# The second layers' sums over d on ScalarE, and three in place of four GpSimd products for the odd streams' third layer

## The chip, the cores and the metric

The kernel runs on one core of a Trainium2 chip. The metric is the device time of one execution in microseconds, with everything from the load of the ids to the store of the result. The profile is one execution of the same program on the chip, and times in it are counted from the start of its span.

## What is computed

A batch of 1024 samples looks up one row of 16 numbers in each of 32 tables (`e`, 1024 x 32 x 16). A compressed interaction network of three layers runs on it, and its sums go with 16 dense features through three dense layers:

```python
x0 = xk = e                                   # b, m = 32, d = 16
for W in (W0, W1, W2):                        # W: 32 x h x 64, h = 32, 64, 64
    xk = relu(einsum('bmd,bhd,mhk->bkd', x0, xk, W))
    outs.append(sum(xk, axis=2))              # the sum over d: b x 64
z = concatenate(outs, axis=1)                 # b x 192
h = relu(concatenate([z, dense_ctx], axis=1) @ W_top1 + b_top1)
h = relu(h @ W_top2 + b_top2)
y = h @ W_top3
```

Everything is float32.

## The kernel before

**Streams and tiles.** The batch is cut into 16 streams of 64 samples (`STREAMS`). Streams 2t and 2t+1 form tile t and share the dense layers; below, a is the even stream of a tile, b the odd one. Even streams use slot 0 of every double buffer, odd ones slot 1 (`s = stream % 2`). The 64 samples times 16 values of d are the 1024 columns of every large tile.

**Layers and chunks.** A layer is a sum over chunks of 128 pairs (m, h): first an elementwise product of `rolled` (rotated copies of x0, 128 x 1024 each, loaded by DMA) and of the layer's input, then two matmuls (one for each half of the columns) of the 64 columns of weights of that chunk, which add up in a PSUM bank of `acc`. The first layer has 4 chunks and one chunk of squares, the second and the third have 16 each. The profile shows four matmul records for a chunk.

**Who makes the products.** VectorE makes most, two chunks at a time into one of three buffers `zd` (128 x 2048 at L406, input `xk_ps` in PSUM); where the number of its chunks in a part is odd, the last instruction has one chunk. GpSimd makes the others, one at a time into four buffers `zg` (L335, input `xk_sb` in SBUF). Between its products GpSimd issues the indirect gathers of the embedding rows (L323), as many after each product as the table `GATHERS_AFTER` says. `CHUNKS[slot, layer]` is a list of parts, each a pair (chunks of VectorE, chunks of GpSimd).

**Order.** The parts are run by TensorE and VectorE in the order of the list `ORDER`. In the steady state a tile t is

```python
ORDER += [(2 * _t - 1, 2, 0), (2 * _t, 0, 0), (2 * _t - 1, 2, 1), (2 * _t, 1, 0), (2 * _t + 1, 0, 0),
          (2 * _t, 1, 1), (2 * _t + 1, 1, 0), (2 * _t, 2, 0)]
```

with entries (stream, layer, part), layers counted from 0. The stream b- = 2t-1 of the tile before finishes its third layer inside this tile. `PLAN.merged` says in which order TensorE takes the products of the two engines. VectorE may be three buffers ahead of TensorE at most: each product waits for `zd_used` of the product three before it.

**After a layer.** ScalarE waits for the layer's last matmul and evacuates `acc` with relu into `xk_ps` and `xk_sb` (L472, four activations of 64 x 512 each), which the next layer's products read (`evacuate`). For the sum over d there are two ways. For the third layers, except that of the last stream, ScalarE makes it itself from PSUM (`sum_d`, L451: 32 activations of 128 x 16 with an accumulated output, each followed by a reading of the accumulator). For the others ScalarE writes relu of the bank to `relu_ab` in SBUF (L481) and VectorE reduces that (L382, `reduce_d`), placed so many products later as `SUMS_AFTER` says for the layer. The function `by_act` says which way a layer goes.

**Banks.** The first layers use bank 2 of `acc`, the second and third layers of a stream use bank s. So the third layer of a stream can't start on TensorE until the second layer's bank has been read for the last time: L563 waits for `relu_ready`, which the L481 activation gives.

**ScalarE's order** is written out by hand from L504: in a tile t copy of the base for a (`base_to_ps`), squares, `sum_d(a - 2)`, evacuate (a, 0), the same for b, then the copies of the dense layers (`zsum_to_sb`, `h1_to_sb`), evacuate (a, 1), `h2_to_sb`, `y_to_sb`, evacuate (b, 1).

## Time and profile before

| what | value |
|---|---|
| median of 3 runs | 620.88 us (619.57 to 621.36) |
| the profiled execution, its time | 619.78 us |
| its span in the profile | 618.0 us |
| TensorE matmuls, share of the span busy | 91% |
| VectorE | 90% |
| GpSimd | 76% |
| ScalarE | 48% |
| granted TensorE clock, mean | 0.994 |

Of two engines that pass buffers to each other, the one that sets the pace is the one that the other waits for. Both TensorE and VectorE are nearly always busy here, so the table alone doesn't say which it is: that is read stretch by stretch from the idle time that stands in square brackets behind the rows of the timeline, with the engine whose work ended it. ScalarE's records of `sum_d` overlap each other in time, so their busy time and mean durations are larger than the time that a sum takes.

### The profile page before, as it was taken

What the parts mean: (1) busy time and instruction counts of PE and PEld (TensorE: products, weight loads), DVE (VectorE), ACT (ScalarE), POOL (GpSimd) and SP (SyncE); (2) the same over time, 40 slices, a digit from 0 to 9 for tenths busy, and PEclk for the clock granted to TensorE, in tenths of its full rate; (3) what the DMA queues carried; (4) which work ended last, traced back from release to release, by engine and by line L of the source; (5) the groups of instructions that cost most, each with busy time, mean ns of one, the idle gap of its engine ahead of it and who ended that gap; (6) DMA issues with size and microseconds to landing.
All of it is one profiled execution on the core that took longest, in us unless ns stands there. A gap on an engine that the chain in (4) does not pass through costs nothing.

```text
span 618.0 us, 8180 instructions
## 1 busy us (share of the span) xinstructions
PE 562.0 (91%) x2752; PEld 206.1 (33%) x2752; DVE 554.5 (90%) x281; ACT 299.5 (48%) x1366; POOL 468.6 (76%) x354
## 2 busy tenths in 40 slices
PE   0058889999999999999999999899998999999997
PEld 0012222334333443334333433234332433334334
DVE  0067899999999999999999999989998999999991
ACT  0021607574357535674366535674346544774331
POOL 6748888888888888888888888888888885125450
PEclk9998999999999999999999999999999999999999
DMA  6297979792699819893699719793498809892000
GB/s 171 79 382 254 394 250 396 241 397 82 209 359 330 294 51 374 297 399 108 218 351 339 299 40 379 265 400 130 171 397 309 329 3 319 316 406 100 1 2 0
DMA packets 54252, 152.02 MB, mean 246 GB/s; under 512 B 9697, under 2 KB 18913, under 8 KB 54210
## 3 DMA queue, kind: packets, MB, share of 16 engines
q1 hardware_dynamic: 46018, 149.39, 64.7%
q0 software_dynamic: 8192, 2.11, 2.6%
q8 instruction: 21, 0.34, 0.2%
q14 instruction: 21, 0.17, 0.1%
HBM read 147.26 MB, written 4.20 MB: 245 GB/s over the span
## 4 chain that ended last, share of the span: by engine, by line
PE 48%; POOL 23%; DVE 10%; issue 9%; DMA 6%; SPq 1%; ACT 1%; DVEq 0%; POOLq 0%
PE acc L570 43%; POOL emb L323 14%; DVE zd L406 10%; POOL zg L335 9%; DMA rolled<-x_scratch 5%; PE mlp L613 2%; SPq L287 1%; PE mlp L604 1%; PE mlp L605 1%; PE acc L579 1%; PE mlp L620 0%; DVE zpart L382 0%; PE mlp L586 0%; ACT xk_sb L472 0%; DMA emb<-tables_in,index 0%
## 5 line engine op out<-in xcount | busy, mean ns | idle before, releaser
L406 DVE TENSOR_TENSOR zd<-rolled,xk_ps 128x2048 f32<-128x2048 f32 x239 | 530.0, 2279 | 16.2 <-PE acc L570 9.2
L570 PE MATMUL acc<-zd,w_sb 128*64 128x512 f32 x1672 | 384.6, 597 | 8.4 <-DVE zd L406 8.4
L323 POOL DMA_INDIRECT emb<-tables_in,index x256 | 244.6, 955 | 75.3 <-issue 64.3
L335 POOL TENSOR_TENSOR zg<-rolled,xk_sb 128x1024 f32<-128x1024 f32 x94 | 223.8, 2382 | 52.0 <-ACT xk_sb L472 18.9
L570 PEld LDWEIGHTS acc<-zd,w_sb 128*64 128x64 f32 x1672 | 119.7, 138 | 242.5 <-issue 210.4
L472 ACT ACTIVATE xk_sb<-acc 64x512 f32<-64x512 f32 x128 | 75.7, 591 | 64.4 <-PE acc L570 61.9
L570 PE MATMUL acc<-zg,w_sb 128*64 128x512 f32 x376 | 98.6, 601 | 6.9 <-POOL zg L335 6.9
L570 PE MATMUL acc<-zd,w 128*64 128x512 f32 x256 | 61.6, 601 | 37.4 <-DVE zd L406 37.4
L472 ACT ACTIVATE xk_ps<-acc 64x512 f32<-64x512 f32 x126 | 71.8, 570 | 30.1 <-PE acc L570 27.2
L451 ACT ACTIVATE relu_ab<-acc 128x16 f32<-128x16 f32 x480 | 78.9, 294 | 8.3 <-PE acc L570 8.3
L451 ACT ACTIVATION_READ_ACCUMULATOR relu_ab<-acc 128x1 f32 x480 | 79.3, 322 | 0.0
L434 ACT ACTIVATE xk_sb<-base 128x1024 f32<-128x1024 f32 x16 | 16.9, 1056 | 67.6 <-PE acc L570 39.2
L570 PEld LDWEIGHTS acc<-zg,w_sb 128*64 128x64 f32 x376 | 26.9, 137 | 58.3 <-issue 41.8
L570 PEld LDWEIGHTS acc<-zd,w 128*64 128x64 f32 x256 | 18.7, 139 | 74.3 <-issue 71.6
L430 ACT COPY xk_ps<-base 128x512 f32<-128x512 f32 x30 | 16.6, 587 | 45.4 <-DVE zd L406 28.2
L406 DVE TENSOR_TENSOR zd<-rolled,base 128x1024 f32<-128x1024 f32 x4 | 4.9, 1225 | 27.9 <-DMA rolled<-x_scratch 27.7
L382 DVE TENSOR_REDUCE zpart<-relu_ab 128x32 f32<-128x512 f32 x33 | 22.3, 677 | 5.2 <-ACT relu_ab L481 5.2
L491 ACT ACTIVATE h<-mlp,bt 128x128 f32<-128x128 f32 x28 | 8.0, 368 | 38.8 <-PE mlp L605 38.8
L481 ACT ACTIVATE relu_ab<-acc 128x512 f32<-128x512 f32 x33 | 19.7, 597 | 9.4 <-PE acc L570 8.6
L502 ACT COPY z2d_y<-mlp 1x128 f32<-1x128 f32 x7 | 1.8, 254 | 36.4 <-PE mlp L620 36.4
L579 PE MATMUL acc<-xk_sb,w 128*64 128x512 f32 x64 | 17.2, 613 | 0.0
L613 PEld LDWEIGHTS mlp<-h,wt 128*128 128x128 f32 x112 | 13.0, 191 | 5.7 <-issue 5.7
(45 smaller groups left out, 101.0 us busy)
## 6 DMA issues: line engine op xcount, KB each, us to landing
rolled<-x_scratch SPq DMA_DIRECT2D x256, 512.0 KB, 9.4
base<-x_scratch SPq DMA_DIRECT2D x16, 512.0 KB
emb<-tables_in,index POOLq DMA_INDIRECT x256
x_scratch<-emb SPq DMA_DIRECT2D x32, 128.0 KB
w_sb<-w_in SPq DMA_DIRECT2D x2, 512.0 KB, 4.9
wt<-wtop_in SPq DMA_DIRECT2D x1, 512.0 KB, 6.3
wt1a<-wtop_in SPq DMA_DIRECT2D x1, 256.0 KB, 5.5
w<-w0a_in SPq DMA_DIRECT2D x1, 160.0 KB, 2.3
```

The source lines that it names most:

```text
L323: pool.indirect_dma_start(emb[:, i % 2, c * DIM:(c + 1) * DIM], None, tables, bass.IndirectOffsetOnAxis(index[:, g:g + 1].bitcast(U32), 0) ...
L335: nc.gpsimd.tensor_tensor(zg[:, n % ZG_BUFS, :], rolled[:, s, j, :], xk_sb[:, s, :], ALU.mult).then_inc(zg_ready, 1)
L382: nc.vector.tensor_reduce(zpart[:, t % 2, layer, s, :], relu_ab[:, s, :].rearrange("p (b d) -> p b d", d=DIM), AX_X, ALU.add).then_inc(red ...
L406: nc.vector.tensor_tensor(zd[:, n % ZD_BUFS, 0:w, :], rolled[:, s, j:j + w, :], repeated(layer_in, w), ALU.mult).then_inc(zd_ready, 1)
L430: nc.scalar.copy(xk_ps[:, s, h * HALF:(h + 1) * HALF], base[:, h * HALF:(h + 1) * HALF]).then_inc(base_ps, 1)
L434: nc.scalar.activation(xk_sb[:, i % 2, :], base[:, :], ACT.Square).then_inc(squares_ready, 1)
L451: end = nc.scalar.activation(relu_ab[:, s, cols], acc[:, s, cols], ACT.Relu, accum_out=zpart[:, t % 2, 2, s, b:b + 1])
L472: nc.scalar.activation(dst[copy * MAPS:(copy + 1) * MAPS, s, h * HALF:(h + 1) * HALF], acc[h * MAPS:(h + 1) * MAPS, bank, :], ACT.Relu).th ...
L481: nc.scalar.activation(relu_ab[:, s, :], acc[:, bank, :], ACT.Relu).then_inc(relu_ready, 1)
L570: end = nc.tensor.matmul(acc[h * MAPS:(h + 1) * MAPS, bank, :], weights, z[:, h * HALF:(h + 1) * HALF], start=(j + c == 0), stop=(i == len ...
L579: nc.tensor.matmul(acc[h * MAPS:(h + 1) * MAPS, bank, :], w0[:, L0CH, :], xk_sb[:, s, h * HALF:(h + 1) * HALF], start=False, stop=False)
L613: end = nc.tensor.matmul(mlp[:, c * TB:(c + 1) * TB], wt2[:, k, c * P:(c + 1) * P], h1[:, k, :], start=(k == 0), stop=(k == H1 // P - 1))
```

## The change

Two things change in one step. First, `by_act` is true of the second layers too: their sum over d is made by `sum_d` on ScalarE, the L481 activation and VectorE's reduction of these 16 layers fall away, and TensorE's third layers wait for `summed` in place of `relu_ready`. Second, the second part of an odd stream's third layer goes from (8, 3) to (9, 2): VectorE makes nine chunks of it, the ninth in an instruction of its own, and GpSimd two. (The last stream has a row of its own in `CHUNKS_AT` and keeps its split, so this is seven streams.) The seven gathers that stood after three products, as 2, 2 and 3, stand after two, as 3 and 4.

```diff
@@ -44,7 +44,7 @@
 
 
 CHUNKS = {(0, 0): [(4, 0)], (0, 1): [(4, 0), (10, 2)], (0, 2): [(12, 4)],
-          (1, 0): [(4, 0)], (1, 1): [(14, 2)], (1, 2): [(4, 1), (8, 3)]}
+          (1, 0): [(4, 0)], (1, 1): [(14, 2)], (1, 2): [(4, 1), (9, 2)]}
 
 CHUNKS_AT = {(0, 1): [(14, 2)], (0, 2): [(6, 1), (8, 1)], (STREAMS - 1, 2): [(12, 4)]}
 
@@ -54,12 +54,12 @@
               (2 * _t, 1, 1), (2 * _t + 1, 1, 0), (2 * _t, 2, 0)]
 ORDER += [(STREAMS - 1, 2, 0)]
 
-SUMS_AFTER = [5, 5, 4]
+SUMS_AFTER = {0: 5, 2: 4}
 
 
 GATHERS_FIRST = 24
 GATHERS_EARLY = 8
-GATHERS_AFTER = {(0, 1, 1): [3, 3], (1, 1, 0): [3, 3], (0, 2, 0): [3, 3, 2, 2], (1, 2, 0): [3], (1, 2, 1): [2, 2, 3]}
+GATHERS_AFTER = {(0, 1, 1): [3, 3], (1, 1, 0): [3, 3], (0, 2, 0): [3, 3, 2, 2], (1, 2, 0): [3], (1, 2, 1): [3, 4]}
 GATHERS_AFTER_AT = {(0, 1, 0): [4, 7], (0, 2, 0): [3], (1, 1, 0): [3, 4], (0, 2, 1): [7],
                     (STREAMS - 1, 2, 0): [0, 0, 0, 0]}
 
@@ -113,12 +113,17 @@
 
 def by_act(stream, layer):
 
-    return layer == 2 and stream < STREAMS - 1
+    return layer > 0 and (stream, layer) != (STREAMS - 1, 2)
 
 
 def sums_to(stream, layer):
 
     return sum(last_part(q) and not by_act(*ORDER[q][:2]) for q in range(end_of(stream, layer) + 1))
+
+
+def act_sums_to(stream, layer):
+
+    return sum(last_part(q) and by_act(*ORDER[q][:2]) for q in range(end_of(stream, layer) + 1))
 
 
 def phase_before(stream, layer):
@@ -438,18 +443,20 @@
                 who, n, _, _ = PLAN.merged[end_of(stream, layer)][-1]
                 act.wait_ge(zd_used if who == "dve" else zg_used, n + 1)
 
-            def sum_d(stream):
-
-                s, t = stream % 2, stream // 2
-
-                act.wait_ge(reduced, sums_to(stream, 1))
+            def sum_d(stream, layer):
+
+                s, t, bank = stream % 2, stream // 2, bank_of(stream, layer)
+
+                act.wait_ge(reduced, sums_to(stream, layer - 1))
+                if layer == 2:
+                    act.wait_ge(summed, act_sums_to(stream, 1))
                 if t > 1:
 
                     act.wait_ge(zsum_done, t - 1)
                 for b in range(SH):
                     cols = slice(b * DIM, (b + 1) * DIM)
-                    end = nc.scalar.activation(relu_ab[:, s, cols], acc[:, s, cols], ACT.Relu,
-                                               accum_out=zpart[:, t % 2, 2, s, b:b + 1])
+                    end = nc.scalar.activation(relu_ab[:, s, cols], acc[:, bank, cols], ACT.Relu,
+                                               accum_out=zpart[:, t % 2, layer, s, b:b + 1])
                 end.then_inc(summed, 1)
 
             def evacuate(stream, layer):
@@ -472,12 +479,12 @@
                                 nc.scalar.activation(
                                     dst[copy * MAPS:(copy + 1) * MAPS, s, h * HALF:(h + 1) * HALF],
                                     acc[h * MAPS:(h + 1) * MAPS, bank, :], ACT.Relu).then_inc(ready, 1)
-                if layer > 0:
-
-                    act.wait_ge(reduced, sums_to(stream, layer - 1))
-                elif stream > 1:
-
-                    act.wait_ge(summed, stream - 1)
+                if by_act(stream, layer):
+                    return
+                before = phase_before(stream, layer)
+                if before:
+
+                    act.wait_ge(summed, act_sums_to(*before))
                 nc.scalar.activation(relu_ab[:, s, :], acc[:, bank, :], ACT.Relu).then_inc(relu_ready, 1)
 
             def zsum_to_sb(m):
@@ -507,29 +514,33 @@
             base_to_ps(1)
             squares(1)
             evacuate(0, 1)
+            sum_d(0, 1)
             evacuate(1, 0)
             evacuate(1, 1)
+            sum_d(1, 1)
             act.wait_ge(const_in, const_count)
             for t in range(1, TILES):
                 a, b, m = 2 * t, 2 * t + 1, t - 1
                 base_to_ps(a)
                 wait_end(a - 2, 2)
                 squares(a)
-                sum_d(a - 2)
+                sum_d(a - 2, 2)
                 evacuate(a, 0)
                 base_to_ps(b)
                 wait_end(b - 2, 2)
                 squares(b)
-                sum_d(b - 2)
+                sum_d(b - 2, 2)
                 evacuate(b, 0)
                 zsum_to_sb(m)
                 h1_to_sb(m)
                 evacuate(a, 1)
                 h2_to_sb(m)
+                sum_d(a, 1)
                 y_to_sb(m)
                 evacuate(b, 1)
+                sum_d(b, 1)
             wait_end(STREAMS - 2, 2)
-            sum_d(STREAMS - 2)
+            sum_d(STREAMS - 2, 2)
             evacuate(STREAMS - 1, 2)
             act.wait_ge(last_z01_done, 1)
             nc.scalar.copy(z01[:, :], stage[:, 0:TB]).then_inc(last_z01_sb, 1)
@@ -558,9 +569,9 @@
                 if layer == 0 and stream > 0:
                     pe.wait_ge(relu_ready, sums_to(stream - 1, 0))
                 elif layer == 1 and part == 0 and stream > 1:
-                    pe.wait_ge(summed, stream - 1)
+                    pe.wait_ge(summed, act_sums_to(stream - 2, 2))
                 elif layer == 2 and part == 0:
-                    pe.wait_ge(relu_ready, sums_to(stream, 1))
+                    pe.wait_ge(summed, act_sums_to(stream, 1))
                 for i, (who, n, j, w) in enumerate(merged):
                     pe.wait_ge(zd_ready if who == "dve" else zg_ready, n + 1)
                     for c in range(w):
@@ -589,8 +600,8 @@
 
             def zsum(m):
 
-                pe.wait_ge(reduced, sums_to(2 * m + 1, 1))
-                pe.wait_ge(summed, 2 * (m + 1))
+                pe.wait_ge(reduced, sums_to(2 * m + 1, 0))
+                pe.wait_ge(summed, act_sums_to(2 * m + 1, 2))
                 if m > 0:
                     pe.wait_ge(y_ready, m)
                 half_sums(m, mlp[0:MAPS, 0:TB], 0)
@@ -625,7 +636,8 @@
             pe.wait_ge(const_in, const_count)
             def last_sums():
 
-                pe.wait_ge(reduced, sums_to(STREAMS - 1, 1))
+                pe.wait_ge(reduced, sums_to(STREAMS - 1, 0))
+                pe.wait_ge(summed, act_sums_to(STREAMS - 1, 1))
                 half_sums(TILES - 1, stage[0:MAPS, 0:TB], 0)
                 half_sums(TILES - 1, stage[MAPS:P, 0:TB], 1).then_inc(last_z01_done, 1)
 
@@ -642,7 +654,7 @@
 
             m = TILES - 1
             pe.wait_ge(last_z01_sb, 1)
-            pe.wait_ge(summed, STREAMS - 1)
+            pe.wait_ge(summed, act_sums_to(STREAMS - 2, 2))
             for c in range(H1 // P):
                 nc.tensor.matmul(last_h1_bank[c], wt1a[:, c * P:(c + 1) * P], z01[:, :], start=True, stop=False)
             pe.wait_ge(y_ready, m)
```

What stands on ScalarE in the first tile, from stream 0's second layer to stream 1's second layer. Before (two `evacuate` blocks, each ended by L481, then the start of the third):

```order
L472 ACTIVATE xk_sb<-acc 64x512 x4
L472 ACTIVATE xk_ps<-acc 64x512 x4
L481 ACTIVATE relu_ab<-acc 128x512
L472 ACTIVATE xk_sb<-acc 64x512 x4
L472 ACTIVATE xk_ps<-acc 64x512 x4
L481 ACTIVATE relu_ab<-acc 128x512
```

After (L458 is `sum_d`, L479 the evacuations, L488 what was L481):

```order
L479 ACTIVATE xk_sb<-acc 64x512 x4
L479 ACTIVATE xk_ps<-acc 64x512 x4
L458 ACTIVATE relu_ab,zpart<-acc 128x16 x32
L479 ACTIVATE xk_sb<-acc 64x512 x4
L479 ACTIVATE xk_ps<-acc 64x512 x4
L488 ACTIVATE relu_ab<-acc 128x512
```

The 32 small activations stand between the evacuation of stream 0's second layer and that of stream 1's first layer, where one activation stood.

What stands on VectorE in one steady turn, from behind the reduction of the first layer of one b to that of the next. Before (the reductions are those of (a, 1), (b, 1), the next (a, 0) and the next (b, 0)):

```order
L406 TENSOR_TENSOR zd<-rolled,xk_ps 128x2048 x5
L382 TENSOR_REDUCE zpart<-relu_ab 128x32
L406 TENSOR_TENSOR zd<-rolled,xk_ps 128x2048 x7
L382 TENSOR_REDUCE zpart<-relu_ab 128x32
L406 TENSOR_TENSOR zd<-rolled,xk_ps 128x2048 x10
L382 TENSOR_REDUCE zpart<-relu_ab 128x32
L406 TENSOR_TENSOR zd<-rolled,xk_ps 128x2048 x8
L382 TENSOR_REDUCE zpart<-relu_ab 128x32
```

After, the same turn (L387 is the reduction, L411 the products):

```order
L411 TENSOR_TENSOR zd<-rolled,xk_ps 128x2048 x21
L411 TENSOR_TENSOR zd<-rolled,xk_ps 128x1024
L387 TENSOR_REDUCE zpart<-relu_ab 128x32
L411 TENSOR_TENSOR zd<-rolled,xk_ps 128x2048 x9
L387 TENSOR_REDUCE zpart<-relu_ab 128x32
```

Of four reductions in the tile two are left, those of the first layers, and one product of half the width is new. It stands before the reduction of (a, 0), at the end of part (b-, 2, 1).

What TensorE takes in the part (b-, 2, 1) and the part (a, 1, 0) behind it (here stand two matmuls for a chunk; `zd` are VectorE's chunks, `zg` GpSimd's), before:

```order
L570 MATMUL acc<-zd,w_sb 64x512 x4
L570 MATMUL acc<-zg,w_sb 64x512 x2
L570 MATMUL acc<-zd,w_sb 64x512 x4
L570 MATMUL acc<-zg,w_sb 64x512 x2
L570 MATMUL acc<-zd,w_sb 64x512 x4
L570 MATMUL acc<-zg,w_sb 64x512 x2
L570 MATMUL acc<-zd,w_sb 64x512 x12
```

and after:

```order
L581 MATMUL acc<-zd,w_sb 64x512 x8
L581 MATMUL acc<-zg,w_sb 64x512 x2
L581 MATMUL acc<-zd,w_sb 64x512 x8
L581 MATMUL acc<-zg,w_sb 64x512 x2
L581 MATMUL acc<-zd,w_sb 64x512 x10
```

TensorE has the same number of chunks; the third product of GpSimd is gone from the place before the last ones, and both that are left come later.

## Rows read from the trace of the kernel before

**Rows 1.** the page, busy time of each engine and its share of the span

```profile
PE 562.0 (91%) x2752; PEld 206.1 (33%) x2752; DVE 554.5 (90%) x281; ACT 299.5 (48%) x1366; POOL 468.6 (76%) x354
```

**Rows 2.** timeline of VectorE, one steady tile; start, duration, what, idle before

```profile
229.13 8.88 DVE L406 TENSOR_TENSOR zd<-rolled,xk_ps 128x2048 f32<-128x2048 f32 x4 [0.48 <-PE acc L570]
237.93 0.68 DVE L382 TENSOR_REDUCE zpart<-relu_ab 128x32 f32<-128x512 f32 x1
238.53 22.05 DVE L406 TENSOR_TENSOR zd<-rolled,xk_ps 128x2048 f32<-128x2048 f32 x10
...
290.26 0.68 DVE L382 TENSOR_REDUCE zpart<-relu_ab 128x32 f32<-128x512 f32 x1
...
298.49 8.88 DVE L406 TENSOR_TENSOR zd<-rolled,xk_ps 128x2048 f32<-128x2048 f32 x4 [0.48 <-PE acc L570]
```

**Rows 3.** timeline of TensorE, one steady tile

```profile
248.66 1.89 PE L570 MATMUL acc<-zd,w 128*64 128x512 f32 x8
...
272.22 1.94 PE L570 MATMUL acc<-zd,w_sb 128*64 128x512 f32 x8 [0.22 <-DVE zd L406]
```

**Rows 4.** timeline of TensorE, its waits for GpSimd in two later tiles

```profile
329.89 1.08 PE L570 MATMUL acc<-zg,w_sb 128*64 128x512 f32 x4 [0.55 <-POOL zg L335]
...
401.10 1.08 PE L570 MATMUL acc<-zg,w_sb 128*64 128x512 f32 x4 [1.67 <-POOL zg L335]
```

**Rows 5.** timeline of VectorE, the same place in the first and last tiles

```profile
159.77 8.88 DVE L406 TENSOR_TENSOR zd<-rolled,xk_ps 128x2048 f32<-128x2048 f32 x4 [0.48 <-PE acc L570]
...
510.58 8.88 DVE L406 TENSOR_TENSOR zd<-rolled,xk_ps 128x2048 f32<-128x2048 f32 x4 [0.48 <-PE acc L570]
...
580.03 8.88 DVE L406 TENSOR_TENSOR zd<-rolled,xk_ps 128x2048 f32<-128x2048 f32 x4 [0.49 <-PE acc L570]
```

**Rows 6.** groups by shape: products and gathers; busy us, mean ns, idle before

```profile
L406 DVE TENSOR_TENSOR zd<-rolled,xk_ps 128x2048 f32<-128x2048 f32 x239 | 530.0, 2279 | 16.2 <-PE acc L570 9.2 <-DMA rolled<-x_scratch 6.3 <-ACT xk_ps L472 0.3
...
L323 POOL DMA_INDIRECT emb<-tables_in,index x256 | 244.6, 955 | 75.3 <-issue 64.3 <-DVE zd L406 6.1 <-DVE index L365 2.6
L335 POOL TENSOR_TENSOR zg<-rolled,xk_sb 128x1024 f32<-128x1024 f32 x94 | 223.8, 2382 | 52.0 <-ACT xk_sb L472 18.9 <-PE acc L570 18.2 <-DMA rolled<-x_scratch 13.2
...
L406 DVE TENSOR_TENSOR zd<-rolled,base 128x1024 f32<-128x1024 f32 x4 | 4.9, 1225 | 27.9 <-DMA rolled<-x_scratch 27.7
```

**Rows 7.** timeline of GpSimd, first wait but issue after 73.69

```profile
503.94 2.37 POOL L335 TENSOR_TENSOR zg<-rolled,xk_sb 128x1024 f32<-128x1024 f32 x1 [0.42 <-PE acc L570]
```

**Rows 8.** timeline of ScalarE, one steady tile, with one sum

```profile
235.69 0.60 ACT L481 ACTIVATE relu_ab<-acc 128x512 f32<-128x512 f32 x1
240.84 1.11 ACT L430 COPY xk_ps<-base 128x512 f32<-128x512 f32 x2 [4.54 <-DVE zd L406]
...
245.54 0.17 ACT L451 ACTIVATE relu_ab<-acc 128x16 f32<-128x16 f32 x1
...
250.45 0.45 ACT L451 ACTIVATION_READ_ACCUMULATOR relu_ab<-acc 128x1 f32 x1
...
290.79 0.62 ACT L497 ACTIVATE h<-mlp,bt 128x128 f32<-128x128 f32 x2 [1.68 <-PE mlp L613]
```

**Rows 9.** timeline of ScalarE, first tile

```profile
69.45 0.60 ACT L481 ACTIVATE relu_ab<-acc 128x512 f32<-128x512 f32 x1
71.17 2.44 ACT L472 ACTIVATE xk_sb<-acc 64x512 f32<-64x512 f32 x4 [1.13 <-PE acc L570]
73.64 2.35 ACT L472 ACTIVATE xk_ps<-acc 64x512 f32<-64x512 f32 x4
```

**Rows 10.** timeline of VectorE, first tile

```profile
76.06 0.68 DVE L382 TENSOR_REDUCE zpart<-relu_ab 128x32 f32<-128x512 f32 x1
76.65 4.47 DVE L406 TENSOR_TENSOR zd<-rolled,xk_ps 128x2048 f32<-128x2048 f32 x2
...
103.61 0.68 DVE L382 TENSOR_REDUCE zpart<-relu_ab 128x32 f32<-128x512 f32 x1
```

**Rows 11.** the chain that ended last, its end

```profile
578.12 26.76 PE acc L570 x124
```

## Prediction

> **What bounds the kernel now.** The page comes first: TensorE is busy for 91% of the span, VectorE for 90%, GpSimd for 76%, ScalarE for 48% [rows 1]. Two engines near 90% that hand buffers to each other can't be told apart by that, so the second view is the timeline of VectorE over one steady tile. It has one place where VectorE waits for TensorE with all three buffers full, 0.48 us before the product at 229.13, and it comes back at 298.49, one tile of 69.36 us later [rows 2]. From there VectorE runs without a gap, and it is TensorE that catches up: its one wait for a product in that tile is at 272.22 [rows 3]. Then TensorE is ahead until the next full point. So each tile has two stretches. From the full point to 272.22 the end is set by VectorE's chain; from 272.22 to the next full point it is set by TensorE alone, and time taken from VectorE there buys nothing.
>
> VectorE's chain can be counted. Ten products start in 238.53 to 260.50, 2.197 us each, and a reduction moves the next start by 0.60 us (237.93 to 238.53) [rows 2]. From 229.13 to the product that TensorE waits for stand 19 products and two reductions: 19 x 2.197 + 1.20 = 42.94, which gives 272.07. TensorE starts at 272.22 [rows 3]. The count holds.
>
> The third view is the same full point over the whole run. From 159.77 to 298.49 two tiles take 69.36 us each, but the six tiles from 159.77 to 580.03 take 420.26 [rows 2, 5], where six of the steady kind would take 416.16. The 4.10 us between them stand on TensorE as waits for GpSimd's third product of part (b-, 2, 1): 0.55 us in tile 4, 1.67 in tile 5 [rows 4], and once more as much in tile 6. GpSimd doesn't wait for anyone from its product at 73.69 to 503.94 [rows 7]: it falls behind slowly, since its gathers (0.955 us plus 0.29 idle) and its products (2.38 us) take more than a tile in tiles 1 to 5 [rows 6]. Behind 578.12 TensorE runs 124 records without a gap [rows 11], so at the end it is the bound, and one chunk (four records) costs it 0.86 us.
>
> **What the change does, part by part.**
>
> *GpSimd, one product fewer in each of seven tiles.* A product with its gap is 2.4 to 2.7 us (2.38 alone; with the mean idle of a gather, 0.29, added [rows 6]); I take 2.5. At the wait of 0.55 us in tile 4 three products are saved, 7.6 us. Against that stands a delay of some 3.4 us that the change brings in the first tile (below), since GpSimd's product there reads what ScalarE writes later. The 4.2 us left exceed 0.55, and a tile later 6.7 exceed 1.67. The waits go: -4.1 us. I give this nearly its full size; the least would be zero.
>
> *VectorE in the steady tiles.* Of the 19 products and two reductions on its chain, one reduction leaves (the one at 237.93, -0.60). The other that leaves stands at 290.26 [rows 2], in the stretch where TensorE sets the end, and brings nothing. The new product of half the width comes on the chain. No row has it with this input. The four single products of the first layer take 1225 ns where a double takes 2279 [rows 6], so a single is 1.054 shorter: 2.197 - 1.054 = 1.14 us. The bounds are 1.05 (the columns alone) and 1.23 (the whole record). Without the reduction VectorE reaches the buffer of the last product of (a, 2) slightly before TensorE has freed it: TensorE ends that part 5 chunks before 248.66, at 244.37 [rows 3], and VectorE would start on that buffer 0.07 us too early. So a tile gets longer by 1.14 - 0.60 + 0.07 = +0.6 us (0.45 to 0.75). Six full tiles lie between 159.77 and 580.03: +3.6 us. The seventh single product is in the first tile.
>
> *ScalarE in the steady tiles.* A sum starts at 245.54 and its last reading of the accumulator starts at 250.45 [rows 8]: 5.0 us for 32 pairs, 5.4 with the end of the last record. The mean durations of these records can't be added, since they overlap. The sum of (b, 1) takes the place of the activation at 235.69 and ends at 240.8 to 241.1. Three things stand behind it: TensorE's part (b-, 2, 0) at 244.37, 3.3 us later; the base copies, which began at 240.84, take 1.1 us and are needed by VectorE seven products after 229.13, at 244.5; and the squares, which wait for TensorE at 244.4 anyway. The sum of (a, 1) starts behind the copy at 290.79 and ends at 296.8; TensorE wants that bank 16 chunks before 244.37, at 230.6, which is 300.0 in this tile, 3.2 us later. Cost in the steady tiles: nothing, with 3 us of cover in each.
>
> *The first tile.* Here there is no such cover. The activation at 69.45 becomes a sum of 5.1 us, and stream 1's evacuation, which began at 71.17 and ended at 75.99 [rows 9], can start only at 74.55 and ends at 79.4. VectorE's part (1, 1, 0) needs it, and began at 76.65 [rows 10]: +2.75 us, with the reduction at 76.06 already taken out. TensorE's (0, 2, 0) is late by three microseconds too, but TensorE was waiting for VectorE in this stretch. From here to the first steady point VectorE's chain sets the pace: the reduction at 103.61 [rows 10] leaves (-0.60) and the first single product comes (+1.14). The sum of (1, 1) ends about 107.5, a microsecond before VectorE needs the base copies behind it. Together +3.3 us (3.1 with the shortest sum and single, 3.8 with the longest).
>
> *The end.* TensorE is the bound and its work is the same: 0.
>
> **Sum.** +3.3 + 3.6 - 4.1 = +2.8 us on the span of 618.0. The profiled execution took 619.78, so 1.78 lie around the span, and 622.6 is its successor. The median of the runs before is 1.10 above the profiled one; so the forecast for the median is 623.7 us.
>
> **What the notes say.** The Trainium skill (Perfetto Trace Analysis, Identifying the Most-Contended Engine) says to take occupancy as the measure and to relieve the engine that has most of it; by that VectorE, with 9.6 us of reductions gone and 8.0 us of single products new, is relieved, by 1.6 us. The first rival below is this rule put to work, and gives 615.2 us where my sum gives 623.7; the trace speaks against it, since the relief at 290.26 falls where VectorE waits. The Trainium skill (ScalarE: Activation LUTs, Rules for kernel authors) budgets about 0.3 us for each ACTIVATE, which would make a sum 10 us; the trace has 5.0, and this rule stands beside the third rival.
>
> **Rivals.**
> 1. *VectorE's total decides.* If what counts is VectorE's whole work and not its place, 16 reductions (16 x 0.60 = 9.6) leave and seven singles (8.0) come: -1.6, and with the GpSimd waits gone -5.7, 615.2 us. It decides if VectorE keeps what it gains at 290.26 over the full point, and if its lead covers the late evacuation of the first tile. Against it: the wait of 0.48 at every full point, and 0.6 us of lead where 2.75 are wanted. Chance 7%.
> 2. *One of the two losses isn't there*: the first tile is covered (3.6 - 4.1), or the tiles keep 69.36 (3.3 - 4.1). Then 620.1 to 620.4 us, no change to be measured. Chance 17%.
> 3. *The sums are late in every tile.* This needs a sum of more than 8.3 us. With 10 us each the two streams wait 1.7 and 1.8 us in each of seven tiles and the first tile loses 5 more: 623.7 + 24 + 5 = 653. For it speaks only that no row shows a sum with other work queued straight behind it. Chance 5%.
> 4. *GpSimd's waits stay*, because it loses its lead again to waits of its own: 623.7 + 4.1 = 627.8. It would have to lose 4 us before tile 4. Chance 4%.
>
> My forecast has the other 67%.
>
> **How the numbers follow.** A difference of 0.3% is 1.9 us, about what a measurement of this kernel can tell. The forecast's own range is 622.2 to 625.2: the bounds of the single product (7 x 0.1), of the sum (0.4) and the scatter of the median (0.9). Rival 2 with some scatter brings the low end to 619.8, and half of rival 4 the high end to 626.3. Faster is rival 1 and a little of rival 2: 0.10. Same is most of rival 2 and a small part of the forecast, whose lower edge lies at 1.3 above the median of before: 0.22. Slower is the rest: 0.68.
>
> **What the new profile would show.** In a steady tile, the full point on VectorE comes back after 69.9 to 70.1 us in all tiles alike, and TensorE has no waits for GpSimd. TensorE's wait for VectorE ahead of (a, 1, 1) is about 0.9 us in two or three pieces in place of 0.22 to 0.38. VectorE's first product of (1, 1, 0) stands at 79.4 behind a wait for ScalarE. GpSimd shows waits from the middle on. I would be wrong if TensorE waits for ScalarE's sum in the steady tiles, if the full points stay 69.4 apart, or if a single product costs about as much as a double.

## The result, and the profile of the changed kernel

The changed kernel took 627.25 us (median of six runs, 624.82 to 629.62), the kernel before beside it 619.91 us (619.11 to 621.36). The ratio is 1.0113, with a 95% interval of 1.0086 to 1.014: slower by 1.1%. The forecast was 623.7 us with a range up to 626.3, so the sign was right and the size was not: 7.3 us lost where 2.8 were forecast. (The 620.88 us of the table above are the median of three of the six executions that give 619.91.) The profiled execution has a span of 625.5 us and took 627.29.

The page of the changed kernel, busy time of each engine, answers to [rows 1]:

```profile
PE 568.2 (91%) x2752; PEld 206.7 (33%) x2752; DVE 553.6 (89%) x272; ACT 377.9 (60%) x2374; POOL 451.4 (72%) x347
```

The work moved as the diff says. ScalarE has 78 us more, GpSimd 17 us less, VectorE about the same. TensorE has the same 2752 matmuls and 6 us more of busy time, a first sign that its clock wasn't always full.

The timeline of VectorE, changed kernel, first tile and its full point, answers to [rows 10] and the first of [rows 5]:

```profile
79.38 4.49 DVE L411 TENSOR_TENSOR zd<-rolled,xk_ps 128x2048 f32<-128x2048 f32 x2 [3.63 <-ACT xk_ps L479]
83.78 0.68 DVE L387 TENSOR_REDUCE zpart<-relu_ab 128x32 f32<-128x512 f32 x1
84.38 24.25 DVE L411 TENSOR_TENSOR zd<-rolled,xk_ps 128x2048 f32<-128x2048 f32 x11
110.10 4.49 DVE L411 TENSOR_TENSOR zd<-rolled,xk_ps 128x2048 f32<-128x2048 f32 x2 [1.47 <-ACT xk_ps L435]
115.32 6.68 DVE L411 TENSOR_TENSOR zd<-rolled,xk_ps 128x2048 f32<-128x2048 f32 x3 [0.74 <-PE acc L581]
...
165.50 29.91 DVE L411 TENSOR_TENSOR zd<-rolled,xk_ps 128x2048 f32<-128x2048 f32 x14 [0.48 <-PE acc L581]
```

The first wait is the one that was forecast, at the forecast time, 79.4. The second (1.47 us, for the base copies behind the sum of (1, 1)) and the third (0.74 us, for TensorE) were not. The full point is at 165.50 where it was at 159.77: 5.73 us lost in the first tile, forecast 3.3.

The same engine's full points in the later tiles, changed kernel, answer to [rows 2, 5]:

```profile
203.36 13.28 DVE L411 TENSOR_TENSOR zd<-rolled,xk_ps 128x2048 f32<-128x2048 f32 x6 [0.43 <-DMA rolled<-x_scratch]
...
306.93 29.80 DVE L411 TENSOR_TENSOR zd<-rolled,xk_ps 128x2048 f32<-128x2048 f32 x14 [1.02 <-PE acc L581]
...
376.83 29.91 DVE L411 TENSOR_TENSOR zd<-rolled,xk_ps 128x2048 f32<-128x2048 f32 x14 [0.48 <-PE acc L581]
...
587.53 4.49 DVE L411 TENSOR_TENSOR zd<-rolled,xk_ps 128x2048 f32<-128x2048 f32 x2 [0.48 <-PE acc L581]
```

The six tiles take 587.53 - 165.50 = 422.03 us, 1.77 more than before; the forecast was 0.5 less. The tile from 306.93 to 376.83 has the forecast length, 69.90 (69.96 was said). Others are longer: the first has two waits for a DMA (0.23 and 0.43 us), and the second ends with a wait for TensorE of 1.02 us in place of 0.48, at 306.93. From the last full point to the end are 37.97 us, as before (618.0 - 580.03).

ScalarE, the sum of (1, 1) in the first tile of the changed kernel (timeline, with the two longest idle times in it and the copy behind it):

```profile
102.32 0.18 ACT L458 ACTIVATE relu_ab<-acc 128x16 f32<-128x16 f32 x1
...
107.47 0.20 ACT L458 ACTIVATION_READ_ACCUMULATOR relu_ab<-acc 128x1 f32 x1 [0.32 <-issue]
...
108.17 0.18 ACT L458 ACTIVATE relu_ab<-acc 128x16 f32<-128x16 f32 x1 [0.50 <-issue]
...
108.96 1.11 ACT L435 COPY xk_ps<-base 128x512 f32<-128x512 f32 x2
```

Sixty-four small instructions stand in a row that wait for nothing that the profile shows, and still ScalarE stands idle between some of them; these gaps are called stops below. The sum takes 108.96 - 102.32 = 6.64 us to the next instruction, where 5.0 to 5.4 were read from [rows 8]. The two stops shown are 0.82 of the 1.25 us that are too many; the rest isn't listed as idle time.

TensorE, its two waits for these sums (timeline) and its granted clock around them (busy time in stretches; the clock is the number behind POOL's):

```profile
74.72 6.02 PE L581 MATMUL acc<-zd,w_sb 128*64 128x512 f32 x16 [4.06 <-ACT relu_ab L458]
...
108.99 2.48 PE L581 MATMUL acc<-zd,w_sb 128*64 128x512 f32 x8 [2.76 <-ACT relu_ab L458]
```

```profile
74.00:78.00 4.00, 3.28 (x8) 1.00 (x10) 1.75 (x1) 3.88 (x15) 0.95 (x1) 0.50 1.03 396
...
108.00:112.00 4.00, 3.01 (x10) 0.97 (x12) 2.53 (x2) 3.81 (x25) 3.54 (x3) 0.78 1.03 398
112.00:116.00 4.00, 4.00 (x18) 1.32 (x16) 3.26 (x3) 3.55 (x45) 3.51 (x4) 0.79 0.34 106
```

Sixteen matmul records take 6.02 us behind a wait of 4.06 us, where sixteen take 3.6 elsewhere. In 74 to 78 the granted clock was 0.50, the lower of its two levels, 1.2 GHz. Behind the second wait it was low in a part of 108 to 116, and there VectorE waited 0.74 us for TensorE.

### The profile page after: what moved, and what is told of

The parts are those of the page before. It is cut to its first block, busy times and chain, and to the rows that moved or that the text cites. A ratio compares the mean times of both kernels' runs of the same rounds, so it can differ in the third digit from the quotient of the medians.

```text
span 625.5 us, 9190 instructions
## 1 busy us (share of the span) xinstructions
PE 568.2 (91%) x2752; PEld 206.7 (33%) x2752; DVE 553.6 (89%) x272; ACT 377.9 (60%) x2374; POOL 451.4 (72%) x347
## 4 chain that ended last, share of the span: by engine, by line
PE 47%; DVE 15%; issue 15%; POOL 14%; DMA 4%; ACT 2%; DVEq 1%; SPq 1%; POOLq 0%
PE acc L581 41%; DVE zd L411 15%; POOL emb L328 9%; POOL zg L340 5%; DMA rolled<-x_scratch 3%; PE mlp L624 2%; PE mlp L615 1%; DVEq L409 1%; ACT relu_ab L458 1%; PE mlp L616 1%; DMA emb<-tables_in,index 1%; ACT xk_sb L479 1%; PE acc L590 1%; PE mlp L597 0%; DMA zg<-w0b_in 0%
## 5 line engine op out<-in xcount | busy, mean ns | idle before, releaser
L411 DVE TENSOR_TENSOR zd<-rolled,xk_ps 128x2048 f32<-128x2048 f32 (+1 forms) x246 | 537.4, 2251 | 24.3 <-PE acc L581 10.7
L581 PE MATMUL acc<-zd,w_sb 128*64 128x512 f32 x1700 | 394.3, 603 | 13.6 <-ACT relu_ab L458 6.8
L340 POOL TENSOR_TENSOR zg<-rolled,xk_sb 128x1024 f32<-128x1024 f32 x87 | 206.9, 2380 | 70.4 <-ACT xk_sb L479 30.1
L458 ACT ACTIVATE relu_ab<-acc 128x16 f32<-128x16 f32 x992 | 163.6, 268 | 7.8 <-issue 4.0
L458 ACT ACTIVATION_READ_ACCUMULATOR relu_ab<-acc 128x1 f32 x992 | 164.9, 294 | 3.0 <-issue 2.5
L479 ACT ACTIVATE xk_sb<-acc 64x512 f32<-64x512 f32 x128 | 75.7, 591 | 69.8 <-PE acc L581 46.4
L581 PE MATMUL acc<-zg,w_sb 128*64 128x512 f32 x348 | 91.1, 600 | 2.3 <-POOL zg L340 2.3
L479 ACT ACTIVATE xk_ps<-acc 64x512 f32<-64x512 f32 x126 | 71.8, 570 | 22.9 <-PE acc L581 17.4
L581 PEld LDWEIGHTS acc<-zg,w_sb 128*64 128x64 f32 x348 | 25.1, 138 | 48.9 <-issue 42.3
L411 DVE TENSOR_TENSOR zd<-rolled,base 128x1024 f32<-128x1024 f32 x4 | 4.9, 1225 | 28.4 <-DMA rolled<-x_scratch 27.1
L387 DVE TENSOR_REDUCE zpart<-relu_ab 128x32 f32<-128x512 f32 x17 | 11.5, 679 | 5.8 <-ACT relu_ab L488 5.8
L488 ACT ACTIVATE relu_ab<-acc 128x512 f32<-128x512 f32 x17 | 10.2, 597 | 9.0 <-PE acc L581 8.6
L624 PE MATMUL mlp<-h,wt 128*128 128x128 f32 x112 | 14.4, 281 | 0.0
```

The costliest lines, as they stand in the source:

```text
L340: nc.gpsimd.tensor_tensor(zg[:, n % ZG_BUFS, :], rolled[:, s, j, :], xk_sb[:, s, :], ALU.mult).then_inc(zg_ready, 1)
L387: nc.vector.tensor_reduce(zpart[:, t % 2, layer, s, :], relu_ab[:, s, :].rearrange("p (b d) -> p b d", d=DIM), AX_X, ALU.add).then_inc(red ...
L411: nc.vector.tensor_tensor(zd[:, n % ZD_BUFS, 0:w, :], rolled[:, s, j:j + w, :], repeated(layer_in, w), ALU.mult).then_inc(zd_ready, 1)
L458: end = nc.scalar.activation(relu_ab[:, s, cols], acc[:, bank, cols], ACT.Relu, accum_out=zpart[:, t % 2, layer, s, b:b + 1])
L479: nc.scalar.activation(dst[copy * MAPS:(copy + 1) * MAPS, s, h * HALF:(h + 1) * HALF], acc[h * MAPS:(h + 1) * MAPS, bank, :], ACT.Relu).th ...
L488: nc.scalar.activation(relu_ab[:, s, :], acc[:, bank, :], ACT.Relu).then_inc(relu_ready, 1)
```

## Experiments

The theory after the result: the mechanism of the forecast holds, and the two sums in the first tile cost more than was forecast for them. What was open was whether they always do, because of the change itself, or whether the 4.5 us beyond the forecast belong to the execution: the stops inside ScalarE's sums, and what TensorE's clock makes of them. The rival to both: another part of the change, the steady tiles or the chunks. The expectations letter their theories A and B; the letters are those of their own group of runs (1 to 4, 5 to 8, 9 and 10). In all kernels below the diff is against the changed kernel unless said otherwise; only the deciding lines are shown. Where a sum goes back to VectorE, the waits on it go back to what they were before, and where a chunk goes back to GpSimd, the gathers stand behind the products as 2, 2 and 3 again. The runs were timed on several chips, each group beside the kernel before on the same chip, so a kernel is compared with that one by its ratio.

**1. The first tile's sums back on VectorE.**

```diff
-    return layer > 0 and (stream, layer) != (STREAMS - 1, 2)
+    return (layer == 1 and (stream > 1)) or (layer == 2 and stream < STREAMS - 1)
```

> Of the changed kernel, the second-layer sums of streams 0 and 1 alone go back to VectorE (with their L481 activations); the other 14 stay on ScalarE and all seven chunks stay moved. Theory A (the first tile is where most of the unforeseen loss lies: the point that I use for tile 1 came 5.7 us later than before, of which the first single product is 1.1): 627.3 - 4.6 = 622.7 us, and VectorE's first product of (1, 1, 0) is back near 76.7. Theory B (the first tile costs only what I forecast, 3.3 us with the single product, and the rest of the loss is spread over the later tiles): 627.3 - 2.2 = 625.1 us.

621.37 us (619.19 to 622.30), ratio 1.0014 [1.0001, 1.0026]. The full point of the first tile is at 160.06, 0.3 us behind that of the kernel before, and four of the six tiles take 70.02. That is below both expectations, nearer to the one that puts the loss on the two early sums. So what the change loses in its first tile comes from the two sums there. The six tiles take 421.54 us, 1.3 more than before, of which 1.2 are waits for a DMA in two of them; without these the longer tiles and GpSimd's relief nearly cancel. How much the two sums cost can't be read from 627.25 - 621.37: the changed kernel wasn't run in this group, and kernel 5 shows how far it differs between groups.

**2. The chunks back, all sums on ScalarE.**

```diff
+def split_moved(stream):
+    return False
+
 def chunks(stream, layer):
+    if stream % 2 and stream < STREAMS - 1 and layer == 2 and not split_moved(stream):
+        return [(4, 1), (8, 3)]
```

> Of the changed kernel, the chunk move alone is undone: GpSimd makes three products of part (b-, 2, 1) again; all second-layer sums are on ScalarE. Theory A (a tile with the single product on VectorE's chain is 0.6 us and more longer; GpSimd, which starts 3.4 us late in the first tile, is the bound in tiles 4 to 6 again): 619.9 + 3.4 = 623.3 us, tiles of about 69.0 us before GpSimd binds, and TensorE waits for GpSimd's third product. Theory B (the tiles are long because of the sums on ScalarE, not because of the single product): tiles stay near 70 and the time stays near 626 to 627 us.

622.73 us (621.94 to 623.12), ratio 1.0036 [1.0020, 1.0052]. The timeline of VectorE, kernel 2:

```profile
162.19 30.98 DVE L420 TENSOR_TENSOR zd<-rolled,xk_ps 128x2048 f32<-128x2048 f32 x14 [0.49 <-PE acc L600]
...
300.39 31.04 DVE L420 TENSOR_TENSOR zd<-rolled,xk_ps 128x2048 f32<-128x2048 f32 x14 [0.48 <-PE acc L600]
...
371.34 19.99 DVE L420 TENSOR_TENSOR zd<-rolled,xk_ps 128x2048 f32<-128x2048 f32 x9 [0.48 <-PE acc L600]
...
513.79 30.98 DVE L420 TENSOR_TENSOR zd<-rolled,xk_ps 128x2048 f32<-128x2048 f32 x14 [0.48 <-PE acc L600]
...
583.23 8.88 DVE L420 TENSOR_TENSOR zd<-rolled,xk_ps 128x2048 f32<-128x2048 f32 x4 [0.48 <-PE acc L600]
```

The timeline of TensorE, its waits for GpSimd in two of these tiles, kernel 2:

```profile
333.05 1.08 PE L600 MATMUL acc<-zg,w_sb 128*64 128x512 f32 x4 [1.66 <-POOL zg L346]
...
404.30 1.08 PE L600 MATMUL acc<-zg,w_sb 128*64 128x512 f32 x4 [1.65 <-POOL zg L346]
```

The first two tiles take 69.1 us each, (300.39 - 162.19) / 2; then GpSimd is late, and three tiles take 71.1, (513.79 - 300.39) / 3. That is the other half of the change seen by itself: without one chunk less on GpSimd, a faster VectorE only meets GpSimd earlier. The time is 0.6 us from the one that the first theory gave.

**3. The chunk alone, no second-layer sum on ScalarE.**

```diff
-    return layer > 0 and (stream, layer) != (STREAMS - 1, 2)
+    return (layer == 1 and (False)) or (layer == 2 and stream < STREAMS - 1)
```

> Of the kernel before, the chunk move alone is made; all second-layer sums stay with VectorE. Theory A (place on VectorE's chain decides): each of six tiles 1.2 us longer (no reduction leaves the chain), the first tile 1.1, GpSimd's 4.1 us of waits gone: 619.9 + 7.2 + 1.1 - 4.1 = 624.1 us, tiles of 70.5. Theory B (GpSimd's relief is worth more than its waits): 620 or less.

623.98 us (622.34 to 624.83), ratio 1.0050 [1.0029, 1.0071]. The timeline of VectorE, kernel 3:

```profile
373.59 8.88 DVE L420 TENSOR_TENSOR zd<-rolled,xk_ps 128x2048 f32<-128x2048 f32 x4 [0.48 <-PE acc L600]
...
444.08 8.88 DVE L420 TENSOR_TENSOR zd<-rolled,xk_ps 128x2048 f32<-128x2048 f32 x4 [0.48 <-PE acc L600]
```

A tile of 70.49 us, where [rows 2] have 69.36: the single product costs 1.13 us on VectorE's chain. The term was 1.14, and the time 0.1 us from what was expected.

**4. Sums from stream 2 on, and the chunk moved only where GpSimd was late.** As kernel 1, and:

```diff
+def split_moved(stream):
+    return stream in (5, 7, 9)
+
 def chunks(stream, layer):
+    if stream % 2 and stream < STREAMS - 1 and layer == 2 and not split_moved(stream):
+        return [(4, 1), (8, 3)]
```

> A version meant to beat both: the second-layer sums are on ScalarE from stream 2 on (streams 0 and 1 as before), and the chunk is moved in streams 5, 7 and 9 alone, where GpSimd's lag builds up. Theory A: three tiles of 69.0 us (TensorE alone is the bound) and three of 69.95, first tile as before, no waits for GpSimd: 416.9 us for six tiles against 420.3, so 619.9 - 3.4 = 616.5 us. Theory B (the tiles have some 0.35 us each of another loss that comes with the sums on ScalarE): 618.5 us.

618.96 us (617.07 to 619.70), ratio 0.9979 [0.9966, 0.9991]: a little faster than before, and 0.5 us above the higher of the two expected times. The timeline of VectorE, kernel 4:

```profile
159.55 30.98 DVE L420 TENSOR_TENSOR zd<-rolled,xk_ps 128x2048 f32<-128x2048 f32 x14 [0.48 <-PE acc L600]
...
577.36 13.27 DVE L420 TENSOR_TENSOR zd<-rolled,xk_ps 128x2048 f32<-128x2048 f32 x6 [0.48 <-PE acc L600]
```

The six tiles take 417.8 us, 577.36 - 159.55. They are of two kinds, 69.0 (the chunk on GpSimd) and 70.0 (on VectorE), with a wait of 0.2 us for the DMA in three of them. So the tiles are those of theory A (416.9 in all), and the loss of 0.35 us in every tile that theory B put behind its 618.5 isn't there. The profiled execution is a fast one, 617.39 us; why the median gains 1.1 us where theory A said 3.4 stays open.

**5. The changed kernel again, unedited, on another chip.**

> The changed kernel itself, unaltered, beside the other kernels of this set. Theory A (the gaps of 0.2 to 0.9 us between the small activations in its first profile belong to the kernel): they stand at the same places, tile 1's full point is again near 165.5, and the time is 627. Theory B (they belong to that execution or that chip): no gaps in the sums, tile 1's full point at 163.3 (the kernel with the chunks back had it at 162.19, plus one single product), 624 to 625 us.

622.60 us (621.78 to 623.64), the kernel before beside it 619.50: ratio 1.0051 [1.0035, 1.0068]. The timeline of VectorE, kernel 5:

```profile
77.48 4.49 DVE L411 TENSOR_TENSOR zd<-rolled,xk_ps 128x2048 f32<-128x2048 f32 x2 [2.90 <-ACT xk_ps L479]
...
106.96 13.28 DVE L411 TENSOR_TENSOR zd<-rolled,xk_ps 128x2048 f32<-128x2048 f32 x6 [0.23 <-ACT xk_ps L435]
...
161.47 29.91 DVE L411 TENSOR_TENSOR zd<-rolled,xk_ps 128x2048 f32<-128x2048 f32 x14 [0.48 <-PE acc L581]
...
512.02 29.91 DVE L411 TENSOR_TENSOR zd<-rolled,xk_ps 128x2048 f32<-128x2048 f32 x14 [0.48 <-PE acc L581]
...
582.04 8.88 DVE L411 TENSOR_TENSOR zd<-rolled,xk_ps 128x2048 f32<-128x2048 f32 x4 [0.48 <-PE acc L581]
```

The base copies are late by 0.23 us in place of 1.47, five of the six tiles take 70.02, and the first of them 70.48 with a DMA wait of 0.38. The same program loses 3.1 us here and lost 7.3 in its first timing. Not all of the 4.03 us between the two full points come from the sums. The timeline of ScalarE, where the sum of (0, 1) starts, first recording and then kernel 5:

```profile
69.06 0.18 ACT L458 ACTIVATE relu_ab<-acc 128x16 f32<-128x16 f32 x1
```

```profile
67.53 0.18 ACT L458 ACTIVATE relu_ab<-acc 128x16 f32<-128x16 f32 x1
```

So 1.53 us stand ahead of the sums, in layers that the change doesn't touch; TensorE's granted clock in 60 to 65 us was 0.75 in the first recording, 0.84 in the kernel before and 1.00 in kernel 5. Counted from the start of this sum to the full point of the first tile, kernel 5 takes 93.94 us and the first recording 96.44. From the activation that stands in its place (69.45, [rows 9]), the kernel before takes 90.32. The undisturbed first tile therefore costs 3.6 us, and the disturbed one 6.1.

The groups of instructions on ScalarE say where the rest comes from (busy, mean ns, idle before). The first recording of the changed kernel:

```profile
L458 ACT ACTIVATION_READ_ACCUMULATOR relu_ab<-acc 128x1 f32 x992 | 164.9, 294 | 3.0 <-issue 2.5
L458 ACT ACTIVATE relu_ab<-acc 128x16 f32<-128x16 f32 x992 | 163.6, 268 | 7.8 <-issue 4.0 <-PE acc L581 3.5
```

and kernel 5, where the 3.7 us are the waits for TensorE ahead of the sums and there is no idle time inside them:

```profile
L458 ACT ACTIVATION_READ_ACCUMULATOR relu_ab<-acc 128x1 f32 x992 | 164.1, 326 | 0.0
L458 ACT ACTIVATE relu_ab<-acc 128x16 f32<-128x16 f32 x992 | 163.4, 299 | 3.7 <-PE acc L581 3.5
```

**6 and 7. One of the two early sums back on VectorE.** The condition of kernel 1 with `stream != 0` (kernel 6) and with `stream != 1` (kernel 7).

> Of the changed kernel, the second-layer sum of stream 0 alone goes back to VectorE. Theory A (stream 0's sum does the harm, since the evacuation of stream 1's first layer stands behind it on ScalarE; stream 1's sum costs TensorE a wait of about 1 us that VectorE's pace hides): tile 1's full point at 159.5 to 160.1, time as with both sums back, 621 us. Theory B (both sums do harm): 623 to 624 us.

> Of the changed kernel, the second-layer sum of stream 1 alone goes back to VectorE. Theory A: the late evacuation costs 2.75 us on VectorE's chain, tile 1's full point at 162.8, time 621.4 + 2.75 = 624.1 us, VectorE's first product of (1, 1, 0) at 79.4 behind ScalarE. Theory B (stream 0's sum costs nearly all): as the changed kernel in this set.

Kernel 6: 621.22 us (618.93 to 622.82), ratio 1.0023 [1.0004, 1.0041]. Kernel 7: 623.34 us (623.26 to 623.67), ratio 1.0060 [1.0043, 1.0076]. Kernel 5, in the same group, had 622.60. Taking the sum of (0, 1) off ScalarE gives 1.4 us by the medians, of four and six executions whose ranges overlap. Taking that of (1, 1) off gives nothing that can be measured, -0.7 by the medians, with DMA waits of 0.22 to 0.52 us in two of kernel 7's tiles. The full points of the first tile are at neither expected place (159.5 to 160.1 for kernel 6, 162.8 for kernel 7). The timeline of VectorE, kernel 6 and then kernel 7:

```profile
161.27 29.91 DVE L420 TENSOR_TENSOR zd<-rolled,xk_ps 128x2048 f32<-128x2048 f32 x14 [0.49 <-PE acc L600]
```

```profile
161.55 29.91 DVE L420 TENSOR_TENSOR zd<-rolled,xk_ps 128x2048 f32<-128x2048 f32 x14 [0.49 <-PE acc L600]
```

Again the time at which the tile is entered differs: stream 0's second layer is evacuated at 70.06 in kernel 6 (granted clock 0.67 in 60 to 65) and at 67.34 in kernel 7 (1.00). From there to the full point kernel 6 takes 91.21 us, kernel 7 94.21 and kernel 5 93.94. So by these recordings, which have no stops, the sum of (0, 1) costs 2.7 us and that of (1, 1) nothing.

**8. TensorE kept busy in its two waits**, by matmuls into a bank that nothing reads then.

```diff
+            def keep_busy(n):
+                for i in range(n):
+                    nc.tensor.matmul(mlp[0:MAPS, :], w12_sb[:, 0, 0, :],
+                                     w12_sb[:, 0, 0:8, :].rearrange("p j k -> p (j k)"), start=True, stop=True)
+
             for q in range(6):
+                if q == 3:
+                    keep_busy(8)
                 phase(q)
             for m in range(TILES - 1):
                 q = 6 + 8 * m
+                if m == 0:
+                    keep_busy(5)
```

> The changed kernel with 8 matmuls of 64 x 512 whose result nobody reads ahead of TensorE's first wait for a ScalarE sum and 5 ahead of the second, in a PSUM bank that is free there. In the first profile TensorE's granted clock was 0.50 from 74 to 78 us and 0.57 from 110 to 114, behind waits of 4.06 and 2.76 us, and the first 16 matmul records behind the first wait took 6.02 us in place of 3.6. Theory A (the slow matmuls behind the first wait are hidden, since VectorE waits for ScalarE till 79.4 anyway; those behind the second delay VectorE's buffers by under 1 us): 0 to 1 us less than the changed kernel in this set, granted clock 1.00 in these stretches. Theory B (the clock is what the forecast missed): 2 us less or more.

626.15 us (624.95 to 629.22), ratio 1.0108 [1.0072, 1.0143]: outside of both. The timeline of TensorE and then of VectorE, kernel 8:

```profile
71.95 6.60 PE L666 MATMUL mlp<-w_sb 128*64 128x512 f32 x15
```

```profile
80.83 4.49 DVE L420 TENSOR_TENSOR zd<-rolled,xk_ps 128x2048 f32<-128x2048 f32 x2 [5.69 <-PE acc L600]
```

The granted clock in 74 to 78 was 1.00, where kernel 5 has 0.57, but each of the eight makes two records of 0.43 us, so they fill 6.6 us of a gap of three, and VectorE waits for TensorE where it waited for ScalarE. The full point comes at 166.50, 5.0 us later than in kernel 5. The test was too coarse: the clock stayed up in this gap while TensorE worked through it, and what that would be worth stays open.

**9. The changed kernel a third time, on a third chip.**

> The changed kernel once more, unedited. Theory A (what the profiled run of the changed kernel showed beyond the forecast, the gaps of 0.3 to 0.9 us between ScalarE's small activations of one sum and the irregular tiles, belongs to a single run and comes and goes): 622 to 623.5 us, the sum of (1, 1) on ScalarE in 5.0 us, full point of tile 1 at about 161.5. Theory B (it belongs to this kernel's longer ScalarE program and returns in part of its runs): 624.5 to 628 us, the sum of (1, 1) in over 6 us, single runs spread over more than 3 us.

624.91 us (623.10 to 627.15), ratio 1.0072 [1.0054, 1.0090], between the two others. The groups on ScalarE, kernel 9:

```profile
L458 ACT ACTIVATION_READ_ACCUMULATOR relu_ab<-acc 128x1 f32 x992 | 165.6, 303 | 2.3 <-issue 2.2
L458 ACT ACTIVATE relu_ab<-acc 128x16 f32<-128x16 f32 x992 | 164.4, 278 | 5.3 <-PE acc L581 3.5 <-issue 1.5
```

The stops are back, 3.7 us in all. The timeline of TensorE, its two waits for the sums of the first tile, kernel 5 and then kernel 9:

```profile
72.95 5.35 PE L581 MATMUL acc<-zd,w_sb 128*64 128x512 f32 x16 [2.97 <-ACT relu_ab L458]
...
105.84 1.94 PE L581 MATMUL acc<-zd,w_sb 128*64 128x512 f32 x8 [1.52 <-ACT relu_ab L458]
```

```profile
74.31 3.65 PE L581 MATMUL acc<-zd,w_sb 128*64 128x512 f32 x16 [1.88 <-ACT relu_ab L458]
...
107.93 3.61 PE L581 MATMUL acc<-zd,w_sb 128*64 128x512 f32 x8 [2.08 <-ACT relu_ab L458]
```

They part the two waits. In kernel 5 the clock is low behind the first alone, and VectorE waits for TensorE nowhere in the tile ahead of 156.50. In kernel 9 it is low behind the second alone, eight records in 3.61 us for 1.94, and VectorE waits 0.36 us for TensorE at 114.25 and 0.25 at 140.49. So the slow matmuls behind the first wait are hidden, and those behind the second are not.

The three profiled executions of one program stand in this order:

| | first | 9 | 5 |
|---|---|---|---|
| idle inside the sums, whole run, us | 6.5 | 3.7 | 0 |
| sum of (0, 1), start to next instruction | 5.47 | 6.06 | 5.01 |
| sum of (1, 1), the same | 6.64 | 5.96 | 5.39 |
| start of the sum of (0, 1) | 69.06 | 68.11 | 67.53 |
| from there to the full point | 96.44 | 96.26 | 93.94 |
| VectorE's wait for the base copies | 1.47 | 0.79 | 0.23 |
| full point of the first tile | 165.50 | 164.37 | 161.47 |
| six tiles | 422.03 | 420.64 | 420.57 |
| span | 625.5 | 623.0 | 620.0 |

Theory B as it was written for this run, that the stops come back in part of the runs, holds in the time and in the spread of 4 us; its sum of over 6 us is 5.96. Theory A, that they belong to a single run, does not hold.

**10. A chunk moved where TensorE sets the pace.** Sums on ScalarE from stream 2 on, the third layers keep (8, 3), and streams 5, 7 and 9 give a chunk of the second layer:

```diff
-CHUNKS_AT = {(0, 1): [(14, 2)], (0, 2): [(6, 1), (8, 1)], (STREAMS - 1, 2): [(12, 4)]}
+CHUNKS_AT = {(0, 1): [(14, 2)], (0, 2): [(6, 1), (8, 1)], (STREAMS - 1, 2): [(12, 4)],
+             (5, 1): [(15, 1)], (7, 1): [(15, 1)], (9, 1): [(15, 1)]}
```

> ScalarE makes the second layers' sums from stream 2 on. The third layer of slot b keeps its three chunks on GpSimd (8, 3); in streams 5, 7 and 9 the second layer of slot b gives one chunk from GpSimd to VectorE, (15, 1) in place of (14, 2), so that VectorE's single product of 1.14 us falls in the stretch of the tile in which VectorE waits for TensorE. If the two stretches of a tile are as I read them: the six tiles at 69.0 us each where GpSimd and DMA don't disturb, 414 to 416 us from the full point of tile 1, and 613.5 to 616 us in all against about 620 before. Rival: VectorE has less slack in that stretch than the product takes (it waited 1.46 us there in tile 4 with the sums gone), or the wait for the DMA at the first-layer product grows: tiles of 69.5 to 70.3 and 617 to 619 us.

620.41 us (618.47 to 622.26), ratio 0.9994 [0.9981, 1.0008]: above both expectations, and its tiles are those of the rival or longer. The timeline of VectorE, kernel 10:

```profile
405.56 2.29 DVE L422 TENSOR_TENSOR zd<-rolled,xk_ps 128x2048 f32<-128x2048 f32 x1 [1.34 <-DMA rolled<-x_scratch]
408.50 13.28 DVE L422 TENSOR_TENSOR zd<-rolled,xk_ps 128x2048 f32<-128x2048 f32 x6 [0.66 <-issue]
```

The queue of SyncE for the same tile, kernel 10 and then kernel 4:

```profile
397.78 0.52 SPq L291 DMA_DIRECT2D base<-x_scratch  x1
```

```profile
395.40 0.52 SPq L289 DMA_DIRECT2D base<-x_scratch  x1
```

That the product costs nothing where it stands now isn't shown: the tiles that have it take 70.41 us (227.75 to 298.16, with 0.4 of a DMA wait) and 70.08 (298.16 to 368.24), no less than kernel 4's 70.0 to 70.3. And then VectorE reaches the next stream's first layer before its rows are there: 2.0 us of idle time at these two products, 1.8 in the next tile. The load of `base` starts 2.4 us later than in kernel 4, and 1.4 of these are already there where the gathered rows are stored (382.93 for 381.52). So the next bound behind this one looks like GpSimd again, by way of its gathers and the loads; no run tests it. This kernel had stops in ScalarE's sums too, 6.0 us in all (three of 0.28 to 0.54 us from 339.47 to 340.90); what part of the result is theirs stays open.

**11 and 12. The kernel before, and kernel 4, on a fourth chip.** Both unedited.

> The kernel before, unedited, beside the version with the later sums on ScalarE. Its ScalarE runs 480 of the small activations, all behind tile 1. If the gaps between them come with the load and not with the number of them: gaps of 0.2 to 0.9 us in its sums too wherever the other kernel of this group shows them; the time stays at 619.5 to 620.5 us, since nothing waits for those sums. If they come with the longer program alone: none here.

> The version with the second layers' sums on ScalarE from stream 2 on and the chunk moved only for streams 5, 7 and 9, once more. Theory B, by which the gaps cost nothing here because the sums of the first tile are not on ScalarE: 616.5 to 619.5 us, a ratio to before of 0.996 to 0.999, gaps or not. Rival: with gaps it loses what the changed kernel lost, 2.5 to 5 us: 621 us or more.

Kernel 11: 620.23 us, ratio 0.9998 [0.9988, 1.0008]. Its groups on ScalarE:

```profile
L451 ACT ACTIVATION_READ_ACCUMULATOR relu_ab<-acc 128x1 f32 x480 | 80.1, 291 | 2.1 <-issue 2.0
L451 ACT ACTIVATE relu_ab<-acc 128x16 f32<-128x16 f32 x480 | 79.4, 267 | 9.6 <-PE acc L570 8.3 <-issue 1.2
```

The kernel before has the stops as well, 3.2 us of them here, and its time doesn't move. Over all the recordings the stops go with the group of runs and not with the program: the first recording (6.5 us) and kernels 9, 10, 11 and 12 (3.7, 6.0, 3.2 and 2.4) have them, and none of kernels 1 to 8, which ran on two other chips; the recording of the kernel before that [rows 8, 9] come from has none either. Whether it is the chip or something else that the runs of a group share isn't known. What counts is whether someone waits for the sum in which they fall. Kernel 12: 619.24 us (617.45 to 621.49), ratio 0.9984 [0.9970, 0.9999], as kernel 4, with 2.4 us of stops in its sums. It is the one version faster than the kernel before in both its timings, by 0.2%.

## Why the prediction was right in sign and wrong in size

*What bounds the kernel.* Right. The two stretches of a tile hold: the single product, placed in VectorE's stretch, costs 1.13 us a tile (kernel 3), the reduction taken from that stretch gives 0.47 (70.49 in kernel 3, 70.02 in kernel 5) where 0.60 less 0.07 was said, and the reduction taken from TensorE's stretch shows up as a longer wait at the same place (0.98 us in kernel 5, 0.38 before) and gives nothing.

*GpSimd's waits, -4.1.* Right. None is left on TensorE in the tiles from 165.50 on in the changed kernel (the one at 57.96, of 2.29 us, stands ahead of the first tile, where the kernel before has 2.62), and kernel 2 brings them back.

*The steady tiles, +3.6.* Right within 0.4 us where nothing disturbs: 70.02 a tile where 69.96 was said, and six of them with the GpSimd term 420.57 and 420.64 in kernels 5 and 9, against 420.26 - 0.5 forecast. TensorE's waits for VectorE in such a tile are 0.35 and 0.26 us (kernel 5), 0.6 where about 0.9 was said. The forecast didn't see the DMA waits, 0.4 us in kernel 5. In the scored recording the six tiles take 422.03, and that is nearly half of the miss: the term was +3.6 - 4.1 and measured +1.8. Of this excess of 2.3 us, 0.86 are DMA waits (0.23, 0.43 and 0.20) and 0.54 the longer wait at 306.93; another 0.4 stand in the tile from 376.83 to 447.21, which has a wait for TensorE of 0.59 us that kernel 5 hasn't. Kernels 5 to 7, without stops, have no such extra wait, and 9 and 12, with stops, have; by what path isn't shown.

*The first tile, +3.3.* The mechanism is right. The 79.38 for 79.4 is in part luck: the sum of (0, 1) started 0.39 us earlier than the activation of [rows 9] and took 5.47 us where 5.1 were said. Without stops the term holds: 3.6 us in kernel 5, by the count from the start of the sum. In the scored recording it is the term that was mis-sized most, at the sentence "The sum of (1, 1) ends about 107.5, a microsecond before VectorE needs the base copies behind it". It ended at 108.96, and VectorE had to wait 1.47 us for the copies. Behind that stood TensorE's lower clock, with 0.74 us and 0.33. The term measured 5.73 us. Even in kernel 5 there is no microsecond of cover: the copies themselves take 1.1 us, and VectorE waits 0.23 for them. Two readings were at fault. The length of a sum was taken from one row of one execution in which the sums ran without a stop, and given a range of 0.4 us. And TensorE was taken for free behind its waits. The forecast speaks of the first, for the sum of (0, 1), and the 2.4 us that sixteen matmul records lose behind it are hidden behind VectorE's own wait, as it said; it has no word on the second, for the sum of (1, 1), where 2.76 us of waiting and the lower clock behind it reach VectorE.

*The scatter.* The range held "the scatter of the median (0.9)", the scatter of the kernel before. The change puts a long sum on the path in the first tile and a second beside it, and with them whatever stops ScalarE has in that run. The kernel before scatters from 619.50 to 620.48 in its medians over five groups; the changed one has 622.60, 624.91 and 627.25. A forecast of 623.7 lies inside these, and the scored timing is the slowest of the three; the range around it was that of another kernel.

*The rivals.* The first (VectorE's total decides) would have been faster, and fell with the wait of 0.98 us at the full point. The Trainium skill (Perfetto Trace Analysis, Identifying the Most-Contended Engine) takes occupancy as the measure of what to relieve; VectorE's busy time went from 554.5 to 553.6 us and the time by 7.3 the other way. The second would have been no change, and neither of its two losses was absent. The fourth had GpSimd's waits stay, and they went. The third (a sum of over 8.3 us) has no row for it: the longest in the changed kernel's first tile is 6.64, the longest in any run 7.1 (kernel 10, at 334.14). The Trainium skill (ScalarE: Activation LUTs, Rules for kernel authors) has about 0.3 us for an ACTIVATE with its bias as a pointer operand; here a pair of small activation and accumulator reading takes 0.157 us.

*What stays open.* What stops ScalarE. The waits are of "issue", the instructions are the same in number, and so are the packets of the two queues that load program code (21 and 29 in the first recording and in kernel 5). Also what the lower clock behind TensorE's second wait would cost without stops: it came only in the two recordings of the changed kernel that have them, and kernel 8 didn't settle it.

## What to carry to other kernels

Before work is moved to an engine that is 48% busy, look for the one place where its consumer has no slack, here the first tile, and leave that place as it was: kernels 4 and 12, with the two early sums left on VectorE and the chunk moved in three streams only, are the ones that gain; kernel 1, which has the first alone, doesn't. An engine that runs long rows of small instructions may be off the path in one version and on it in the next, and then its own scatter becomes the kernel's: give a forecast that puts it there a wider range, on the slow side. When a change relieves one bound and loads another, give back only where the relief is needed (three streams, not seven), and expect the next supplier, here it seems the gathers and loads, within a microsecond or two per tile.

## What the runs showed of the hardware

- ScalarE stops inside rows of small activations (128 x 16, each with a reading of the accumulator) for 0.15 to 1.06 us at a time in some executions, and in others never: 6.5, 3.7, 6.0, 3.2 and 2.4 us in the first recording and kernels 9 to 12, none in kernels 1 to 8. It was seen in the kernel before (kernel 11) as in the changed one. Without stops 32 pairs take 5.0 us, 0.157 each, though the records' means are 299 and 326 ns: the records overlap.
- TensorE's granted clock fell behind some waits and not behind others of the same length, so the length of a wait alone didn't decide it. Behind 4.41, 4.06 and 2.97 us (kernel 2, the first recording, kernel 5) sixteen matmul records took 5.35 to 6.02 us, with a granted clock of 0.67, 0.50 and 0.57 in 74 to 78; behind 2.08 us (kernel 9) eight took 3.61. Behind 1.88 and 2.20 us (kernels 9 and 7) sixteen took 3.65, and behind 1.52 us (kernel 5) eight took 1.94. Ahead of a first layer it fell behind 3.00 us (kernel 9, eight in 2.98) and not behind 2.77 and 3.51 (kernels 5 and 7, eight in 1.94). Behind one and the same wait of 3.85 us, ahead of 46 us, the granted clock of 44 to 54 was 0.83 in kernel 9 and 1.00 in kernel 5.
